# ScalarE makes five of sixteen one-hot matrices, and GpSimd's wait moves behind a gather

## The reference

```
e = stack([tbl_f[ids[:, f]] for f in range(40)], axis=1)
z = einsum('bie,fie,bif->bi', e[:, rowidx], param, e[:, colidx])
h = relu(concat([z, dense_ctx]) @ W_top1 + b_top1)
y = relu(h @ W_top2 + b_top2) @ W_top3
```

## Time and profile before

| | |
|---|---|
| median of 3 runs | 1225.22 us (1223.64 to 1227.79) |
| the profiled execution | 1226.64 us, its span 1224.8 us |
| TensorE busy | 1199.0 us, 98% |
| VectorE busy | 1091.6 us, 89% |
| ScalarE busy | 936.9 us, 76% |
| GpSimd busy | 582.1 us, 48% |

### The profile page before, as it was taken

The page is one execution under the profiler, slowest core; times in us unless marked ns, Lnnn a source line. Parts: engine busy times, 40 slices in busy tenths (PEclk is TensorE's granted clock), DMA queues, the critical chain, the costliest instruction groups (busy, mean ns, idle before and its releaser), DMA issues.

```text
span 1224.8 us, 21870 instructions
## 1 busy us (share of the span) xinstructions
PE 1199.0 (98%) x5772; PEld 429.0 (35%) x5772; DVE 1091.6 (89%) x982; ACT 936.9 (76%) x7308; POOL 582.1 (48%) x623
## 2 busy tenths in 40 slices
PE   8989999998999999999999999999999999999999
PEld 2333333333333333333333333333333333333323
DVE  8779999998998888899998888899999888889990
ACT  0249979897768966899875976989867896689872
POOL 5655565666666565666543546566616352000000
PEclk9999999999999999999999999999999999999999
DMA  3124222232222222222222222222223222111100
GB/s 114 41 65 144 70 75 73 73 76 64 67 73 66 63 56 69 69 65 75 73 60 55 64 60 66 65 75 73 68 56 76 53 59 56 43 48 49 50 12 1
DMA packets 50716, 78.44 MB, mean 64 GB/s; under 512 B 13800, under 2 KB 14056, under 8 KB 50464
## 3 DMA queue, kind: packets, MB, share of 16 engines
q1 hardware_dynamic: 30872, 56.81, 15.4%
q0 software_dynamic: 19712, 20.22, 8.3%
q10 hardware_dynamic: 8, 0.01, 0.0%
HBM read 76.98 MB, written 0.01 MB: 63 GB/s over the span
## 4 chain that ended last, share of the span: by engine, by line
PE 80%; DVE 9%; ACT 6%; issue 4%; DMA 0%; SPq 0%; DVEq 0%; ACTq 0%
PE ring L650 27%; PE ring L656 21%; PE z_ps L669 14%; PE aux L572 6%; ACT act_prod L468 6%; DVE prod L564 4%; PE aux L615 3%; PE ring L572 2%; PE aux L605 2%; DVE act_prod L564 2%; DVE sums L513 2%; PE aux L579 2%; DVE dve_prod L564 1%; PE ring L680 1%; PE aux L586 1%
## 5 line engine op out<-in xcount | busy, mean ns | idle before, releaser
L468 ACT ACTIVATE act_prod<-act_prod 128x64 f32<-128x64 f32 x3584 | 856.5, 244 | 66.2 <-DVE act_prod L564 65.6
L468 ACT ACTIVATION_READ_ACCUMULATOR act_prod<-act_prod 128x1 f32 x3584 | 683.0, 191 | 0.0
L564 DVE TENSOR_TENSOR prod<-ring,emb 128x1024 f32<-128x1024 f32 x448 | 518.0, 1217 | 45.2 <-PE ring L651 44.7
L419 POOL DMA_INDIRECT stage<-tbl,idx x384 | 362.3, 943 | 311.4 <-issue 168.5
L650 PE MATMUL ring<-emb,raw 64*128 64x512 f32 x896 | 438.6, 611 | 13.7 <-DVE prod L564 4.4
L651 PE MATMUL ring<-emb,raw 64*128 64x512 f32 x896 | 438.8, 611 | 0.0
L656 PE MATMUL ring<-raw,emb 64*128 64x512 f32 x704 | 361.7, 621 | 2.8 <-issue 1.5
L657 PE MATMUL ring<-raw,emb 64*128 64x512 f32 x704 | 361.9, 622 | 0.0
L564 DVE TENSOR_TENSOR act_prod<-ring,kept 128x1024 f32<-128x1024 f32 x224 | 263.4, 1219 | 36.7 <-PE ring L657 35.9
L419 POOL DMA_INDIRECT kept<-tbl,idx x232 | 219.0, 944 | 136.4 <-issue 101.9
L650 PEld LDWEIGHTS ring<-emb,raw 64*128 64x128 f32 x896 | 153.7, 186 | 240.9 <-issue 137.8
(11 more groups left out here) (47 smaller groups left out, 329.4 us busy)
## 6 DMA issues: line engine op xcount, KB each, us to landing
raw<-param_b SPq DMA_DIRECT2D x200, 256.0 KB
stage<-tbl,idx POOLq DMA_INDIRECT x384
kept<-tbl,idx POOLq DMA_INDIRECT x232, 2.5
W<-W1g SPq DMA_DIRECT2D x1, 1792.0 KB
act_prod<-tbl SPq DMA_DIRECT2D x6, 224.0 KB
W<-W2t SPq DMA_DIRECT2D x1, 512.0 KB
idx<-ids_t SPq DMA_DIRECT2D x1, 240.0 KB, 5.3
act_prod<-tbl SPq DMA_DIRECT2D x6, 26.0 KB
```

Of the source, the lines that this page charges most:

```text
L419: pool.indirect_dma_start(to[:, t, E * (f % 2) : E * (f % 2) + E], None, tables[f], bass.IndirectOffsetOnAxis(ap=idx[:, c, f, t : t + 1], ...
L468: op = act.activation(part, part, ACT.Copy, accum_out=sums[:, t, at : at + 1])
L564: dve.tensor_tensor(to, ring[:, n % RING, :, :], by, ALU.mult).then_inc(prod_done, 1)
```

## The change

There are two parts. First, matrices 3, 5, 9, 11 and 15 of each of the three duos (ACT_ONES, all of side 1) are made by ScalarE: it copies the ids of side 1 from PSUM to scratch (three copies, all waited for), and for each matrix takes |id - code| (Abs with a bias from less, the negated codes) and then Relu(1 - that). The Abs writes one of two scratch places, so the Abs of matrix n+1 waits for the Relu of matrix n-1. After its first Relu of duos 1 and 2 it saves the duo before. VectorE makes the other eleven. Along with this the ids come in two loads, one for each side, at partitions 0 to 2 and 64 to 66; hot_rows and the cast lie there too, and the spreading matmuls read three rows at those places.

Second, in the first chunk GpSimd waits for the last duo's landing behind the first gather of the next duo, not ahead of it.

```diff
+ACT_ONES = [3, 5, 9, 11, 15]
...
-        hot_ids_i = h1.bitcast(I32)[0 : 2 * len(HOT), 2, :]
-        hot_ids_f = h1[0 : 2 * len(HOT), 3, :]
-        hot_rows = h1[0 : 2 * len(HOT), 0:2, :].rearrange("p a n -> p (a n)").rearrange("p (j n) -> p j n", n=P)
+        def hot_side(side):
+            return slice(E * side, E * side + len(HOT))
+
+        hot_ids_i = h1.bitcast(I32)[:, 2, :]
+        hot_ids_f = h1[:, 3, :]
+        hot_rows = h1[:, 0, :].rearrange("p (j n) -> p j n", n=P)
+
+        def act_ids(j):
+            return dve_prod[0:PIECE, j, 1, :]
+
+        def act_tmp(n):
+            return dve_prod[0:PIECE, n % 2, 0, :]
...
-            sp.dma_start(hot_ids_i, hot_ids).then_inc(ids_loaded, 16)
+            for side in range(2):
+                sp.dma_start(hot_ids_i[hot_side(side)], hot_ids[side]).then_inc(ids_loaded, 16)
...
-                    if n and i == 0:
+                    if n and i == (0 if c else 1):
                         _, landed_last, times_last = staged(*GATHERS[n - 1])
                         pool.wait_ge(landed_last, 16 * 2 * BT * (times_last + 1))
...
+            for j in range(len(HOT)):
+                act.wait_ge(ids_spread, 2 * j + 2)
+                act.activation(act_ids(j), spread_id(j, 1)[0:PIECE], ACT.Copy).then_inc(act_ids_copied, 1)
+            act.wait_ge(act_ids_copied, len(HOT))
+            act.wait_ge(codes_negated, 1)
+            for n in range(len(HOT) * len(ACT_ONES) + 1):
+                if n < len(HOT) * len(ACT_ONES):
+                    j, m = divmod(n, len(ACT_ONES))
+                    k = ACT_ONES[m] // 2
+                    if n >= 2:
+                        act.wait_ge(act_ones, n - 1)
+                    act.activation(act_tmp(n), act_ids(j), ACT.Abs, bias=less[0:PIECE, k : k + 1]).then_inc(act_offs, 1)
+                if n == 0:
+                    continue
+                j, m = divmod(n - 1, len(ACT_ONES))
+                i = ACT_ONES[m]
+                if j and i == 2 * PIECES - 1:
+                    act.wait_ge(aux_ready, AUX_NO["duo", 0, HOT[j - 1]] + 1)
+                elif j:
+                    act.wait_ge(hot_used, (2 * PIECES - 1) * (j - 1) + i + 1)
+                act.wait_ge(act_offs, n)
+                act.activation(one_hot(1, i // 2), act_tmp(n - 1), ACT.Relu, bias=1.0, scale=-1.0).then_inc(act_ones, 1)
+                if j and m == 0:
+                    save_aux("duo", 0, HOT[j - 1])
...
+            for side in range(2):
+                rows = hot_side(side)
+                dve.tensor_copy(
+                    hot_rows[rows], ident[rows, E * side : E * side + BT].unsqueeze(2).to_broadcast([len(HOT), BT, P])
+                ).then_inc(rows_made, 1)
+            dve.wait_ge(ids_loaded, 16 * 2)
+            for side in range(2):
+                dve.tensor_copy(hot_ids_f[hot_side(side)], hot_ids_i[hot_side(side)]).then_inc(ids_cast, 1)
...
+            dve.tensor_scalar(less[:], codes[:], -1.0, None, ALU.mult).then_inc(codes_negated, 1)
             for j in range(len(HOT)):
                 for k, side in product(range(PIECES), range(2)):
                     i = 2 * k + side
+                    if i in ACT_ONES:
+                        continue
...
-                pe.matmul(spread_id(j, side), hot_rows[:, 2 * j + side, :], hot_ids_f, start=True, stop=True).then_inc(
-                    ids_spread, 1
-                )
+                pe.matmul(
+                    spread_id(j, side), hot_rows[hot_side(side), j, :], hot_ids_f[hot_side(side)], start=True, stop=True
+                ).then_inc(ids_spread, 1)
```

More of the change, by code:

```diff
@@ L259, in fm_mlp_kernel @@
         codes = sb("codes", [P, PIECES])
+        less = sb("less", [P, PIECES])
         ring = ctx.enter_context(nc.psum_tensor("ring", [P, RING, 2, CH], F32))
@@ L272, in fm_mlp_kernel @@
         codes_made = sem("codes_made")
-        hot_made = sem("hot_made")
+        codes_negated = sem("codes_negated")
+        dve_ones = sem("dve_ones")
+        act_ones = sem("act_ones")
+        act_offs = sem("act_offs")
+        act_ids_copied = sem("act_ids_copied")
         hot_used = sem("hot_used")
@@ L475, in _ @@
                     for kind, c, i in AUX_AT.get(u, ()):
-                        save_aux(kind, c, i)
+                        if (kind, c) != ("duo", 0) or i not in HOT[:-1]:
+                            save_aux(kind, c, i)
                     if u in SUM_AT:
@@ L532, in _ @@
                         dve.wait_ge(hot_used, (2 * PIECES - 1) * (j - 1) + i + 1)
-                    if k == 0:
-                        dve.wait_ge(ids_spread, 2 * j + side + 1)
+                    if k == 0 and side == 0:
+                        dve.wait_ge(ids_spread, 2 * j + 1)
+                    elif k == 0:
+                        dve.wait_ge(act_ids_copied, j + 1)
                     dve.tensor_scalar(
                         one_hot(side, k), spread_id(j, side)[0:PIECE], codes[0:PIECE, k : k + 1], None, ALU.is_equal
-                    ).then_inc(hot_made, 1)
+                    ).then_inc(dve_ones, 1)
             dve.memset(sums[:], 0.0).then_inc(sums_zero, 1)
@@ L603, in spare_bank @@
                     for k, side in product(range(PIECES), range(2)):
-                        pe.wait_ge(hot_made, 2 * (PIECES * j + k) + side + 1)
+                        i = 2 * k + side
+                        if i in ACT_ONES:
+                            pe.wait_ge(act_ones, len(ACT_ONES) * j + ACT_ONES.index(i) + 1)
+                        else:
+                            before = sum(1 for x in ACT_ONES if x < i)
+                            pe.wait_ge(dve_ones, (2 * PIECES - len(ACT_ONES)) * j + i - before + 1)
                         mm = pe.matmul(
@@ L675, in sum_batch @@
                     mm.then_inc(group_summed, 1)
-            pe.wait_ge(rows_made, 1)
-            pe.wait_ge(ids_cast, 1)
+            pe.wait_ge(rows_made, 2)
+            pe.wait_ge(ids_cast, 2)
             for j, side in product(range(len(HOT)), range(2)):
-                pe.matmul(spread_id(j, side), hot_rows[:, 2 * j + side, :], hot_ids_f, start=True, stop=True).then_inc(
-                    ids_spread, 1
-                )
+                pe.matmul(
+                    spread_id(j, side), hot_rows[hot_side(side), j, :], hot_ids_f[hot_side(side)], start=True, stop=True
+                ).then_inc(ids_spread, 1)
             pe.wait_ge(consts_made, 3)
@@ L775 @@
         "ids_t": np.ascontiguousarray(ids.reshape(NCH, BT, P, FIELDS).transpose(2, 0, 3, 1)),
-        "hot_ids": np.ascontiguousarray(ids[:CH, hot_fields].T),
+        "hot_ids": np.ascontiguousarray(ids[:CH, hot_fields].reshape(CH, len(HOT), 2).transpose(2, 1, 0)),
         "param_b": param_b.reshape(NB, P, BATCH * P),
```

## The result

The changed kernel takes 1219.97 us (median of 7 runs, 1219.68 to 1221.57) against 1225.22 (1223.64 to 1227.79). The ratio is 0.9953, 95% interval 0.9943 to 0.9962: about 5.3 us, or 0.47%, faster. That lies in the range, and is 1.9 us more than the 3.4 us forecast. The profiled execution took 1219.68 us, its span 1217.9.

What follows compares the result with a forecast made beforehand. TensorE was taken to bound the kernel (98% busy, nearly the whole head's chain). Ids +0.8, spreading -5.1, stall +0.9 gave -3.4 us: 1223.2 for the profiled execution, 1221.8 as median, range 1219.0 to 1226.2.

Steps and rivals of the forecast that it cites:

- Start and pairing: Head: two id loads start TensorE 0.8 us later; paired spreading passes save 5.37 us, freeing it at 9.57 instead of 13.89.
- Stall at matrix 3: Duo 0: TensorE reaches matrix 3 at 11.3 and waits for ScalarE till 12.2, giving back 0.9 us.
- The clock in duo 0: TensorE's clock rises 6.0 us after the first pass (gain 3.9) or after the stall (2.6); 3.4 taken.
- Duos 1 and 2 are TensorE's alone: Head: ScalarE's matrices come in time with 0.5 us margin, so 7.14 and 7.07 us stay.
- VectorE's relief is worth nothing by itself: Head: VectorE keeps ahead of TensorE making the matrices, so lifting work off it gains nothing by itself.
- GpSimd's wait: First chunk: moving it saves 1.25 us per duo boundary; worth 0 by itself, but without it most of 3.4 is lost.
- The row at 140.36: Profile before: TensorE turns duo 13 at 140.36, the gather behind its landing starts at 140.78; read as no room.
- The sum: Whole kernel: ids +0.8, spreading -5.1, stall +0.9, together -3.4 us; faster 0.42, same 0.50, slower 0.08.
- spreading did overlap: Rival in the head: spreading does not overlap, TensorE is free at 14.7, head ends 0.8 later, 1226.0 us; chance 0.12.
- the queued gather did not delay landings: Rival in the first chunk: a queued gather delays the landing before it, leaving 0.5 to 1 us, 1224.5; chance 0.07.
- one table load: Rival on ScalarE: Abs and Relu need different tables, a matrix costs 3.9 us, whole 1252 us; chance 0.02.

Runs made afterwards that it cites:

- u_unpaired: Changed kernel, but ids come in one load and all six spreading matmuls read the same six rows: 1223.98 us, ratio 0.9983.
- after_fill2: Changed kernel plus 12 matmul instructions of no use where TensorE idles, run on the later chip: 1218.84 us, ratio 0.9956.
- gather_only: Kernel before with only GpSimd's wait moved: 1223.58 us, ratio 0.9989.
- u_vec_all: Changed kernel, but VectorE makes all sixteen matrices of each duo and ScalarE none: 1222.64 us, ratio 0.9973.
- u_no_gather: Changed kernel, but in the first chunk GpSimd again waits ahead of the next duo's first gather: 1225.11 us, ratio 0.9993.
- before_fill2: Kernel before plus 12 matmul instructions of no use where TensorE idles, run on the later chip: 1223.97 us, ratio 0.9993.
- gather_fill: Kernel before with GpSimd's wait moved and the 12 matmul instructions of no use added: 1222.46 us, ratio 0.9979.

## Why the prediction was right, and where its size was off

- **Start and pairing**: shown. TensorE starts at 4.18 (said 4.20), the passes go in pairs, and it is free at 9.60 (said 9.57). u_unpaired shows that without the pairing there is no gain in the head.
- **Stall at matrix 3**: shown, 11.36 to 12.24, 0.88 us (said 0.9). One matrix costs 1.27 (said 1.33): the Relu's constants come cheaper than the 0.69 of the earlier trace rows, and the wait for itself costs 0.03.
- **The clock in duo 0**: the forecast took 3.4, between gains of 2.6 and 3.9. The clock rose 5.9 us after the first pass, which is the case given as 3.9, and the head gained 4.0. In other executions it rose 3.4 us after it (12.9 in after_fill2, 17.3 in gather_only). So this term varies by itself, in both kernels, by some 1.4 us: that the profiled pair had it alike, 6.0 and 5.9, was luck.
- **Duos 1 and 2 are TensorE's alone**: shown, 7.14 and 7.07.
- **VectorE's relief is worth nothing by itself**: in keeping with u_unpaired, whose head gains nothing; but by u_vec_all it is what makes 1.5 us of the head's 4.0 possible. The prediction did not say what the pairing would be worth without it.
- **GpSimd's wait**: "Worth by itself 0; without it, most of 3.4 would be lost." The second half is shown by u_no_gather, in whose trace 3.4 us of the shift are lost ahead of unit 91. The first half is the term that was off: the wait is worth 1.5 us by itself (before_fill2 to gather_fill; 1.3 without filling), of which the traces show 0.8. The row at 140.36 was read as if every execution had TensorE there at that time. It came from a late one; in the earlier one that was traced TensorE waits. The landing was also put near 128, 12.5 us earlier, and came by 124.99.
- **The sum**: forecast 3.4; measured 5.3 in the medians. Without lowered stretches it is 5.1, of which 1.5 is the wait and 3.6 the head (4.4 in the head of the two traces, 4.1 at their end). The sum had the head nearly right and the wait's own gain at nothing. A gain over 0.3%, which came out, had a chance of 0.42; with 1.5 us more in the sum it would have been the likelier side.
- **The rivals**: spreading did overlap; the queued gather did not delay landings (the hole shrank from 2.3 to 1.0 us, as one issue of 1.25 us should have it); there is one table load, at 0.74. The Trainium skill (ScalarE: Activation LUTs, Table sets: the hidden batching unit) says that abs, relu and copy are in every set, and the trace agrees: 15 Abs and 15 Relu without a load between them.

Open: what held the engines on the slow chip, and whether it hits the changed kernel harder for a reason of its own (1610.89 to 1616.76 against 1559.69). Where 0.7 us of the moved wait's 1.5 arises. Why the lowered stretches come in some executions and not in others, and whether it is by chance that the changed kernel's seven runs had at most one each.

## What to carry to other kernels

A slack of zero in one profile can be a wait in another execution of the same kernel. Before a transfer is priced at nothing, set the profiled time against the median: if the execution is a late one, its slack is too large. And when the bound of a stage is halved, go through the engines that were hidden behind it again: here VectorE's 10.5 us a duo was covered by 10.6 us of spreading, and without ScalarE's five matrices it would have taken back 1.5 us of the head's 4.0 (u_vec_all).

## What the runs showed of the hardware

- Six float32 matmuls of three rows, at partitions 0 and 64 in turn, ran two at a time: 5.49 us, where six of six rows at one place took 10.57 (u_unpaired).
- Ten microseconds of matmuls over six rows did not raise TensorE's clock; after the first pass over 125 rows it rose within 3.4 to 6.0 us, differently from execution to execution of nearly the same program (3.4 in gather_only, 3.8 in before_fill2, 6.0 in the profile before).
- One stretch of 3.4 us at the lower clock costs the kernel before 1 to 2 us of the whole (1.7 and 1.5 in its trace). In most executions it follows idle times of TensorE of 1.64 and 1.77, or of 2.97 us, and these are what brings it: filled with 12 matmuls of no use, all 11 runs of the kernel before stayed at 1.000, where 44 of its 51 runs had not.
- A ScalarE instruction that waits for the one just ahead of it starts 0.03 us after that one's end.
